# A Mamba block and a routed FFN on one core: the first tile's order of work changed from the router's transposes to the first store and load

## What is computed

```python
h = x * rsqrt(mean(x*x) + EPS) * norm_scale
xs, res = split(h @ w_in, 2);  res = silu(res)
xs = silu(causal_depthwise_conv(xs, conv_w, conv_b))        # K = 4
delta, B, C = split(xs @ w_xproj, [16, 32])
delta = softplus(delta @ w_dt + b_dt)
A = -exp(A_log);  state = exp(delta*A) * state + (delta*xs)*B   # a scan over time
y = sum_n(state * C)
x = layernorm(x + x + ((y + xs*D) * res) @ w_out)
x = layernorm(x + shared(x) + routed_top2_of_8(x))
```

## Time and profile before

| | us |
|---|---|
| median of 3 runs | 1852.48 |
| the three runs | 1858.13, 1852.48, 1833.6 |
| the profiled execution | 1853.4 |
| its span, first to last instruction | 1851.6 |

### The profile page before, as it was taken

How to read it: one execution, slowest core, us unless ns; L and a number is a source line. 1 busy time by engine, 2 the same in 40 slices (tenths; PEclk the granted TensorE clock), 3 DMA queues, 4 the chain that set the end, 5 groups by cost and what they waited for, 6 DMA issues and landing times.

```text
span 1851.6 us, 24478 instructions
## 1 busy us (share of the span) xinstructions
PE 1519.8 (82%) x6945; PEld 972.3 (53%) x6946; DVE 1275.8 (69%) x2199; ACT 945.0 (51%) x1795; POOL 894.1 (48%) x416
## 2 busy tenths in 40 slices
PE   4368688797898897898898776876999999999980
PEld 2122133442543543453543432565999999999970
DVE  3068999999999999999999999731333333333326
ACT  2377667468667668657668554321333333333323
POOL 0276875776776876876875876210111111111114
PEclk9679897898898998887997978987999999999995
DMA  4364452453463453453542552266555555555538
GB/s 141 89 154 101 108 142 53 114 137 80 116 144 74 122 140 70 125 137 70 129 122 70 123 128 62 73 200 237 174 174 190 175 178 191 173 188 178 175 120 270
DMA packets 136952, 252.14 MB, mean 136 GB/s; under 512 B 15314, under 2 KB 68419, under 8 KB 136755
## 3 DMA queue, kind: packets, MB, share of 16 engines
q1 hardware_dynamic: 130402, 233.49, 45.3%
q0 software_dynamic: 6480, 17.83, 2.6%
HBM read 205.76 MB, written 45.51 MB: 136 GB/s over the span
## 4 chain that ended last, share of the span: by engine, by line
PE 46%; DVE 29%; ACT 11%; issue 7%; DMA 2%; SPq 1%; POOL 0%; DVEq 0%; ACTq 0%; POOLq 0%
DVE psH L1020 16%; PE psP L1530 13%; PE psH L1519 13%; DVE big L1029 6%; PE psP L1367 4%; PE psP L1356 3%; PE psA L1462 2%; PE psA L1443 2%; PE psP L1382 2%; PE psP L1427 2%; ACT psH L880 2%; ACT L880 1%; PE psP L1399 1%; PE psA L1453 1%; PE psP L1507 1%
## 5 line engine op out<-in xcount | busy, mean ns | idle before, releaser
L464 POOL TENSOR_TENSOR big<-big,B 128x2048 f32<-128x2048 f32 x128 | 578.7, 4530 | 232.0 <-PE psA L1462 147.5
L880 ACT ACTIVATE psH<-big,A_q 128x512 f32<-128x512 f32 x512 | 352.1, 691 | 186.7 <-DVE big L1029 178.2
L1020 DVE TENSOR_TENSOR_SCAN psH<-psH,big 128x512 f32<-128x512 f32 x256 | 311.6, 1218 | 81.8 <-POOL big L464 43.1
L1029 DVE TENSOR_TENSOR big<-psH,C 128x512 f32<-128x512 f32 x512 | 343.1, 670 | 0.0
L1020 DVE TENSOR_TENSOR_SCAN psH<-psH,carry,big 128x512 f32<-128x512 f32 x256 | 326.6, 1276 | 14.0 <-ACT psH L880 13.9
L504 POOL DMA_INDIRECT con_dram<-eo,dest x71 | 68.0, 957 | 481.0 <-ACT eo L932 473.1
L1462 PE MATMUL psA<-big,gsum 128*32 128x512 f32 x1024 | 237.9, 683 | 72.8 <-DVE big L1029 72.8
L1519 PEld LDWEIGHTS psH<-nTb,ew_s 128*128 128x128 f32 x2272 | 266.3, 193 | 4.1 <-issue 0.6
L1519 PE MATMUL psH<-nTb,ew_s 128*128 128x128 f32 x2272 | 266.7, 276 | 0.2 <-issue 0.2
L1530 PE MATMUL psP<-big,hT 128*128 x1136 | 259.0, 381 | 1.0 <-DVE eb L1270 0.7
L1530 PEld LDWEIGHTS psP<-big,hT 128*128 128x128 f32 x1136 | 211.7, 191 | 28.0 <-issue 1.8
(11 more groups left out here) (166 smaller groups left out, 1610.8 us busy)
## 6 DMA issues: line engine op xcount, KB each, us to landing
ew_s<-in_L_ffn_ew_dram SPq DMA_DIRECT2D x71, 1024.0 KB, 4.8
big<-ud_dram SPq DMA_DIRECT2D x128, 512.0 KB, 8.6
ud_dram<-ud SPq DMA_DIRECT2D x32, 512.0 KB, 2.7
xb<-rows_dram SPq DMA_DIRECT2D x71, 130.0 KB, 2.1
B<-bc_dram SPq DMA_DIRECT2D x128, 64.0 KB, 6.0
C<-bc_dram SPq DMA_DIRECT2D x128, 64.0 KB, 7.0
big<-in_L_ffn_ew_dram SPq DMA_DIRECT2D x8, 1024.0 KB, 12.0
big<-con_dram SPq DMA_DIRECT2D x16, 512.0 KB, 8.8
```

The lines of the kernel that those rows point to most:

```text
L464: nc.gpsimd.tensor_tensor(X[:, Q % NX], rep[:, g % 2, 1], B4[:, f:f + 1, :].broadcast_to([P, NR, TC]), ALU.mult).then_inc(bx_ready, 1)
L880: nc.scalar.activation(psH[:, r, :], rep[:, g % 2, 0, r, :], ACT.Exp, scale=A_q[:, c, r, f:f + 1]).then_inc(dA_ready, 1)
L1020: nc.vector.tensor_tensor_scan(psH[:, r, :], psH[:, r, :], X[:, Q % NX, r, :], start, ALU.mult, ALU.add).then_inc(scan_done, 1)
L1029: nc.vector.tensor_tensor(X[:, Q % NX, r, :], psH[:, r, :], C4[:, f, :], ALU.mult).then_inc(hc_ready, 1)
```

## The change

In the first tile only:

- PE: the router's transposes (and their wait for `s_rw`) move from ahead of `PE_FIRST` to behind it.
- ACT: Silu is applied to each chunk of `xs` as it is read, with a semaphore `s_xs0`, in place of one Silu over the four chunks behind the last; PE's X waits chunk by chunk. The Sqrt for the 28 later subtiles moves from ahead of Silu to behind the softplus. Ln, 1+e and (1+e)-1 are made for chunk 0 and then for chunk 1, in place of once for both.
- DVE: the four operations of `input_chunk(0, 0)` move here from POOL. The sign of A now stands ahead of them, the reciprocal behind them.
- POOL: waits for DVE's last one (`u_ready`), counts `sp_pool` up by 3, and does only `input_chunk(0, 1)`.
- SP: `store_ud(0, 0)`, `load_rep(0, 0)`, `load_c(0, 0)`, `store_ud(0, 1)`, the other C loads, `load_rep(0, 1)`.

```diff
@@ gpsimd
-            for c in range(2):
-                input_chunk(0, c)
+            pool.wait_ge(u_ready, 1)
+            pool.sem_inc(sp_pool, 3)
+            input_chunk(0, 1)
@@ sync
             store_ud(0, 0)
-            store_ud(0, 1)
             sp.wait_ge(s_bn, NSUBS - NSUB)
             load_rep(0, 0)
-            for f in range(NF):
+            load_c(0, 0)
+            store_ud(0, 1)
+            for f in range(1, NF):
                 load_c(0, f)
             load_rep(0, 1)
@@ scalar
                 if c + 2 < CH:
                     read_in(0, c + 2)
-            act.wait_ge(s_ms, 2)
-            nc.scalar.activation(rstd1[:, NSUB:], rstd1[:, NSUB:], ACT.Sqrt).then_inc(s_root, 1)
-            silu_xs(0)
+                evacuated(act, 0, ("C", c))
+                nc.scalar.activation(xs[:, 0, c], xs[:, 0, c], ACT.Silu).then_inc(s_xs0 if c < CH - 1 else xs_ready, 1)
...
             dt_exp(0, 0)
-            dt_ln(0, 0)
-            dt_one_plus(0, 0)
-            dt_less_one(0, 0)
+
+            act.wait_ge(sp_act, 3)
+            nc.scalar.activation(ud[:, 0, 1], spe[:, 0], ACT.Ln, bias=1.0).then_inc(s_first, 1)
+            nc.scalar.activation(ud[:, 0, 0], spe[:, 0], ACT.Copy, bias=1.0).then_inc(s_first, 1)
+            act.wait_ge(s_first, 2)
+            nc.scalar.activation(ud[:, 0, 0], ud[:, 0, 0], ACT.Copy, bias=-1.0).then_inc(s_first, 1)
+            nc.scalar.activation(ud[:, 1, 1], spe[:, 1], ACT.Ln, bias=1.0).then_inc(sp_act, 1)
+            nc.scalar.activation(ud[:, 1, 0], spe[:, 1], ACT.Copy, bias=1.0).then_inc(sp_act, 1)
+            act.wait_ge(sp_act, 5)
+            nc.scalar.activation(ud[:, 1, 0], ud[:, 1, 0], ACT.Copy, bias=-1.0).then_inc(sp_act, 1)
+            act.wait_ge(s_ms, 2)
+            nc.scalar.activation(rstd1[:, NSUB:], rstd1[:, NSUB:], ACT.Sqrt).then_inc(s_root, 1)
@@ vector
             dve.wait_ge(s_root, 2)
+            nc.vector.tensor_scalar(A_q[:], A_q[:], -1.0, None, ALU.mult).then_inc(s_neg, 1)
+            dve.wait_ge(s_first, 3)
+            nc.vector.tensor_tensor(spe[:, 0], spe[:, 0], ud[:, 0, 0], ALU.subtract).then_inc(s_u0, 1)
+            nc.vector.tensor_tensor(spr[:, 0], spr[:, 0], ud[:, 0, 1], ALU.add).then_inc(s_u0, 1)
+            dve.wait_ge(s_u0, 2)
+            nc.vector.tensor_tensor(ud[:, 0, 0], spr[:, 0], spe[:, 0], ALU.add).then_inc(s_u0, 1)
+            dve.wait_ge(s_u0, 3)
+            dve.wait_ge(xs_ready, 1)
+            nc.vector.tensor_tensor(ud[:, 0, 1], ud[:, 0, 0], xs[:, 0, 0], ALU.mult).then_inc(u_ready, 1)
+            dve.wait_ge(s_root, 3)
             nc.vector.reciprocal(later, later).then_inc(s_rstd, 1)
-            dve.wait_ge(s_root, 3)
-            nc.vector.tensor_scalar(A_q[:], A_q[:], -1.0, None, ALU.mult).then_inc(s_neg, 1)
@@ tensor
-            pe.wait_ge(s_rw, 16)
-            for d in range(DC):
-                ins = nc.tensor.transpose(psS[:, d * E:(d + 1) * E], rw[:, d * P:(d + 1) * P], ident[0:E, 0:E])
-            ins.then_inc(rwT_full, 1)
...
-                pe.wait_ge(xs_ready, k + 1)
+                if k:
+                    pe.wait_ge(xs_ready, k + 1)
                 for c in range(CH):
+                    if k == 0:
+                        pe.wait_ge(*((s_xs0, c + 1) if c < CH - 1 else (xs_ready, 1)))
...
             for use, i in PE_FIRST:
                 WORK[use](0, i)
+            pe.wait_ge(s_rw, 16)
+            for d in range(DC):
+                ins = nc.tensor.transpose(psS[:, d * E:(d + 1) * E], rw[:, d * P:(d + 1) * P], ident[0:E, 0:E])
+            ins.then_inc(rwT_full, 1)
```

More of the change, by code:

```diff
@@ L253, in build @@
         s_rstd = sem("s_rstd")
+        s_xs0 = sem("s_xs0")
+        s_first = sem("s_first")
+        s_u0 = sem("s_u0")
         s_A = sem("s_A")
```

## The result

The changed kernel took 1819.5 us (median of 4 runs, 1814.98 to 1824.13), the kernel before 1853.28 (4 runs). The ratio is 0.9837, its 95% interval 0.9802 to 0.9872: 30.2 us less, between 23.7 and 36.7 (the two medians alone differ by 33.8). The forecast was 29.5, and the whole interval lies within 2%. In a later session with more runs the ratio was 0.984 (0.9803 to 0.9877). The profiled execution took 1814.98, its span is 1813.2, which is 38.4 less than the span of before.

A forecast was written before the change was run, and what follows sets the result against it. DVE, then PE, bound the long part; ahead of it lies one latency chain. Six terms sum to 29.5 us, shifting the profiled 1853.4 to 1823.9, about 1824; the range for 8 in 10 was 1804 to 1838.

The forecast's parts named there:

- 1 router later: PE's front: transposes of x no longer wait for the router's weights, starting at 9.65 instead of 24.59; 14.94 us less.
- 2 Silu and projection: From convolutions' end to projection's read: chunkwise Silu lets PE run on, 3.5 us for 10.25; 6.7 us less.
- 3 softplus by chunk: ACT's softplus steps: one chunk takes 1.8 us where two together took 3.09; 1.3 us less.
- 4 sums on DVE: Chunk 0's four operations take 2.8 us on DVE where POOL took 5.25; 2.45 us less.
- 5 load behind its store: On SP, the first load follows chunk 0's store directly, 2.64 us behind instead of 5.57; 2.9 us less.
- 6 the load's own time: First load takes 12.39 us instead of 13.63 without chunk 1's store ahead in the queue; 1.2 us less.
- start of the scans: Landing of the first load_rep, when ACT's first decay and POOL's first product begin: 29.5 us earlier, at 65.9.
- The two lower bounds: Projection at the lower clock: term 4.2 instead of 6.7 us; w_out landing at 12.9, not 12.4: 0.3 less.
- One sign named ahead: From POOL's first product to the end, the changed profile would take 1756 us as before.
- Not slower: Rival at SP's queue: the second load delays later transfers, needing 30 us more lateness to exceed 1853; chance 0.02.
- the rival of an absorbed gain: Ahead of the scans, the late x or four weights come last at a fixed time, giving 1839; chance 0.03.
- the second rival: In the scans, PE's lower clock falls elsewhere and runs differ: below 1815.4, down to 1804; chance 0.22.

The follow-up runs named there:

- attempt with PE kept busy: Changed kernel with chunk 0's exponential before chunk 1's read, first load in halves, and twelve unused PE products behind the router's transposes; 1806.92 us, ratio 0.9772.
- delay: Changed kernel with a chain of 60 memsets on DVE ahead of chunk 0's last product, delaying the start by 39.1 us; ratio 1.0043.
- router alone: Kernel before with only PE's transposes of the router's weights moved behind PE_FIRST; ratio 0.9939.
- attempt at more: Changed kernel with chunk 0's exponential before chunk 1's read and the first load in halves, softplus times xs first; medians 1813.5 and 1810.15 us, ratio 0.9776.
- without router: Changed kernel with the router's transposes ahead of PE_FIRST again; ratio 0.9916.
- Silu and projection alone: Kernel before with Silu and the x projection chunk by chunk, the Sqrt and A's sign moving with them; ratio 0.9971.
- SP's order of before: Changed kernel with both stores of ud issued ahead of the first load again; ratio 0.9869.
- sums on POOL: Changed kernel with the four operations for chunk 0 back on POOL instead of DVE; median 1824.57 us, ratio 0.9879.
- second load later: Changed kernel with the shared expert's weights, 2 MB, issued ahead of the second load of ud; median 1823.72 us, ratio 0.9871.
- PE busy: Changed kernel with twelve added unused products on PE behind the router's transposes, ahead of the scans; ratio 0.9799.

## Why the prediction was right, step by step

| step | forecast, us | measured, from the two timelines |
|---|---|---|
| 1 router later | 14.94 | 14.7 (end of the convolutions 50.94, now 36.23); PE's first products 14.9 earlier; the starts of its own two experiments 14.5 and 14.4 |
| 2 Silu and projection | 6.7 | 6.65 (10.25, now 3.60); alone 6.5 |
| 3 softplus by chunk | 1.3 | 1.28 (3.09, now 1.81) |
| 4 sums on DVE | 2.45 | 2.48 (5.25, now 2.77); taken back 2.4 |
| 5 load behind its store | 2.9 | 2.85 (5.57, now 2.72); taken back 3.2 |
| 6 the load's own time | 1.2 | 1.0 (13.68, now 12.66); taken back 1.0 |
| start of the scans | 29.5 | 29.0 |

Each term came from a row of the same operation, or from one that the trace had in another place (a later load, a convolution's row at the full clock). The two lower bounds, for the clock and for a weight that lands late, were not needed: the products by w_in started at 12.66, and the projection's rows took 0.45. But step 1 had nothing to spare, and that it came out nearly whole is in part luck. Over the eleven profiles without the router's wait w_out landed between 0.33 us before ACT had read the transposes and 0.23 behind it, and in four the trace names the weight as what ended the wait, as in the attempt with PE kept busy:

```profile
12.77 6.37 PE L1383 MATMUL psP<-xnT,w_in_s 128*128 128x512 f32 x8 [1.08 <-DMA w_out_s<-in_L_attn_w_out_dram]
```

A faster way to the transposes would find these weights in front of it. The time agrees with the sum less closely than the start does: the later session gives 0.984, but a median of 4 to 6 runs moves by some microseconds, and 1819.5 lies just inside the forecast's 1819 to 1829. One sign named ahead didn't hold: from the first product to the end the changed profile took 1746.8 us, not 1756 as before; the last section is about these 9 us.

The Trainium skill's drain behind a table load (ScalarE: Activation LUTs, "What ACT_TABLE_LOAD costs") doesn't show here either: Silu's first piece began 1.29 us after the start of the load (25.10, 26.39), and the chunk's convolution was then waited for.

Not slower, and not through the second load: it landed 16.1 us after the start, as worked out, inside its cover. The delay shows that the shift reaches the end, within 10 us in 39; the ratio, 30 us less, agrees. The rival of an absorbed gain was wrong in its main part, but had a true grain: with the router alone the late x was in the way for 1 us, and the four weights came within a few tenths of being so.

What failed is the reason that the second rival was given. The spread between runs was put down to PE's lower clock in the scans as well as to the runs themselves. The lower clock exists, but the last section shows another cause for most of the spread between the profiles.

## What to carry to other kernels

A long chain of waits ahead of a stage that is bound by an engine was worth its full length here, as far as the times can tell, and its terms added up; read such a chain backwards from the first instruction of the bound stage and price each wait by the row that ends it. Then ask what stands just behind each wait, and by how much: here a weight and the late x did, within 0.3 and 1 us. A small load at the back of a queue of large ones (the router's weights behind 3.5 MB) belongs ahead of nothing that the first stage needs. When what is left is a transfer in front of two readers, let it land in the order in which they need it.

## What was unexpected: a small operation on DVE can wait for a whole operation on POOL

From the first scan to the table of blocks the same instructions took 1126.9 to 1146.5 us in the fourteen profiles, and the rest, behind the table, 604.5 to 607.9. The spread between executions lies in the scans. Two profiles of one session, at the same place of the program; first DVE and POOL in the changed kernel (that session's profile):

```profile
316.90 0.18 DVE L1167 RECIPROCAL wsum<-wsum 128x4 f32<-128x4 f32 x1
317.12 4.49 DVE L1171 TENSOR_TENSOR xrow<-picked,wsum 128x8 f32<-128x8 f32 x1
...
317.08 8.97 POOL L467 TENSOR_TENSOR big<-big,B 128x2048 f32<-128x2048 f32 x2 [1.29 <-DMA big<-ud_dram]
```

and in the attempt at more:

```profile
312.04 0.17 DVE L1182 TENSOR_TENSOR xrow<-picked,wsum 128x8 f32<-128x8 f32 x1
...
312.39 8.99 POOL L471 TENSOR_TENSOR big<-big,B 128x2048 f32<-128x2048 f32 x2 [1.67 <-DMA big<-ud_dram]
```

The same product of 8 elements a partition took 0.17 us where it began 0.35 us ahead of POOL's product, and 4.49 where it began 0.04 behind it; it ended with POOL's first product, of 4.5 us. Of its eight executions, each profile has some of the one and some of the other kind:

```profile
L1150 DVE TENSOR_TENSOR xrow<-picked,wsum x8: 173/2192/4437, 353.2 to 1241.3; 128x8 f32<-128x8 f32 x8
```

```profile
L1171 DVE TENSOR_TENSOR xrow<-picked,wsum x8: 172/174/4300, 317.4 to 1202.7; 128x8 f32<-128x8 f32 x8
```

(one line's instructions, duration in ns as least/median/most; before, and the changed kernel). A fraction of a microsecond in when DVE gets there decides over more than 4 us.

This holds without exception. Of this product's 112 executions in the fourteen profiles, 43 took 4 us or more, and each of them began 0.03 to 0.42 us behind the start of a product on POOL; of the 29 short ones that began within half a microsecond of such a start, all began ahead of it, by 0.05 to 0.48. And of all DVE operations of at most 256 elements in the scans, the 477 that took over 0.06 us more than their line's shortest all began while an operation of POOL ran, and ended 0.02 to 0.28 us behind the end of one. I summed the 165 small DVE operations (4 to 192 elements a partition) of the scans in each profile:

| profile | first scan to table, us | small operations, us | DVE idle, us |
|---|---|---|---|
| before | 1146.5 | 87.2 | 97.5 |
| changed | 1137.2 | 76.6 | 98.7 |
| changed, second session | 1140.6 | 81.3 | 97.4 |
| router alone | 1130.3 | 73.0 | 95.5 |
| without router | 1146.5 | 87.1 | 97.8 |
| Silu and projection alone | 1140.7 | 80.7 | 98.3 |
| SP's order of before | 1139.8 | 80.5 | 97.3 |
| sums on POOL | 1140.7 | 80.6 | 98.4 |
| delay | 1132.4 | 78.8 | 92.3 |
| second load later | 1143.4 | 82.8 | 99.1 |
| attempt at more (two) | 1133.4, 1133.0 | 72.2, 72.8 | 95.2, 98.5 |
| PE busy | 1136.1 | 79.8 | 94.6 |
| attempt and PE busy | 1126.9 | 69.0 | 92.5 |

Over all fourteen the two first columns go together (correlation 0.94, a slope of 1.03). What is left of each length, the rest of DVE's work, is 961.3 to 962.0 us in twelve of them (966.0 and 965.4 in the first attempt and in the last row), so nearly all of the spread lies in the two columns on the right: 18 us in the small operations, 7 in DVE's idle time. The rival, PE's clock, would show in that idle time. Its mean in the scans ran from 0.87 to 0.89 and was lowest in the two longest, but these two idled no longer than others (97.5 and 97.8); a part in the 7 us isn't excluded. The 9 us by which the profiled execution of the change did better than its start explains are these: 1146.5 less 1137.2 is 9.3, and the small operations are 10.6 shorter. From the first scan on it is the same program in both; only the moments differ. The Trainium skill (SBUF — State Buffer, "SBUF: two separate sides") has a rule that fits: a pair of SBUF ports shared by DVE and GpSimd is an exclusive lock for a whole instruction, taken by DVE operations in a two-port mode, or with two SBUF inputs against a GpSimd operation that reads SBUF. The rows agree, the scans and products with an input in PSUM among them, which keep their 1.19 to 1.29 and 0.66 to 0.69 us beside POOL's products. That a small operation waits for POOL's whole one is what the rows show; that the lock is the reason rests on the page. No run here was made to test it, by moving these small operations away from POOL's; that it explains the spread of the medians too is argued from the profiles, not shown.
